# Query, key, gate and up products in two row tiles, value products in one run, and an order table for each engine

## What is computed

```
q, k, v = xn @ Wq.T, xn @ Wk.T, xn @ Wv.T        # 16 heads of 16 features
attn = softmax(causal(q @ k.T) / 4)              # for each head, 512 x 512
s = (attn @ v) @ Wo.T
h = silu(xn @ wg.T / 127) * (xn @ wu.T / 127)    # 768 features, int weights
g = silu(h @ wd.T / 127)
out = x + s * g
```

## Time and profile before

| what | value |
|---|---|
| median of 3 runs | 946.51 us (945.27 to 947.13) |
| span of the profiled execution | 945.8 us |
| PE busy | 914.8 us (97%), 9065 matmuls |
| DVE busy | 707.2 us (75%) |
| ACT busy | 585.8 us (62%) |
| POOL busy | 495.1 us (52%) |
| DMA queue of the kernel, share of 16 engines | 41.8%, 132.47 MB |

### The profile page before, as it was taken

How to read it: one execution, slowest core, us unless ns; L and a number is a source line. 1 busy time by engine, 2 the same in 40 slices (tenths; PEclk the granted TensorE clock), 3 DMA queues, 4 the chain that set the end, 5 groups by cost and what they waited for, 6 DMA issues and landing times.

```text
span 945.8 us, 22760 instructions
## 1 busy us (share of the span) xinstructions
PE 914.8 (97%) x9065; PEld 685.6 (72%) x9065; DVE 707.2 (75%) x950; ACT 585.8 (62%) x796; POOL 495.1 (52%) x681
## 2 busy tenths in 40 slices
PE   3999999999999999999999999999999999999995
PEld 2777767776868777686877868777786867768654
DVE  5985868778696887868788786877778697776823
ACT  5356664757576675756657575665757557575771
POOL 4253553736456464645636455473745547364553
PEclk9999999999999999999999999999999999999999
DMA  6704235353353534535343453534345253543323
GB/s 221 213 25 170 84 116 169 100 198 132 134 164 127 170 106 179 154 125 171 129 151 126 170 152 117 176 132 158 130 148 162 104 185 120 175 131 135 118 93 98
DMA packets 84507, 133.97 MB, mean 142 GB/s; under 512 B 13680, under 2 KB 34928, under 8 KB 84336
## 3 DMA queue, kind: packets, MB, share of 16 engines
q1 hardware_dynamic: 84400, 132.47, 41.8%
HBM read 53.22 MB, written 25.75 MB: 83 GB/s over the span
## 4 chain that ended last, share of the span: by engine, by line
PE 91%; DVE 2%; DMA 2%; POOL 2%; issue 1%; ACT 1%; SPq 0%; POOLq 0%; ACTq 0%; DVEq 0%
PE bank L194 48%; PE values L525 15%; PE bank L434 12%; PE bank L492 11%; PE bank L447 4%; DMA o_reciprocals<-scratch_r 1%; ACT probs L500 1%; DVE row_max L457 1%; PE bank L463 1%; POOL o_compact L566 1%; PE bank L668 0%; DMA scratch_r<-sum_reciprocals 0%; DVE x_in L259 0%; DVE xt_lo L279 0%; DMA sums<-scratch_o 0%
## 5 line engine op out<-in xcount | busy, mean ns | idle before, releaser
L457 DVE TENSOR_REDUCE row_max<-bank 128x2 f32<-128x768 f32 (+3 forms) x352 | 384.9, 1124 | 63.5 <-PE bank L447 60.3
L500 ACT ACTIVATE probs<-bank 128x1024 f32<-128x1024 f32 x320 | 320.4, 1026 | 122.2 <-PE bank L492 120.8
L507 POOL TENSOR_SCALAR_AFFINE_SELECT probs<-probs 128x256 f32<-128x256 f32 (+1 forms) x448 | 194.0, 450 | 275.1 <-ACT probs L500 274.1
L525 PE MATMUL values<-probs,v 128*17 128x512 f32 (+3 forms) x2048 | 166.2, 436 | 0.9 <-POOL probs L507 0.9
L393 POOL TENSOR_TENSOR h_lo<-gated,h_hi 128x512 fp32r<-128x512 f32 x96 | 124.6, 1298 | 74.8 <-ACT h_hi L390 72.7
L434 PE MATMUL bank<-k_stack,q_stack 64*128 64x128 f32 (+3 forms) x1024 | 155.3, 363 | 1.5 <-DVE row_max L457 1.2
L492 PE MATMUL bank<-q_stack,k_stack 64*128 64x512 f32 (+3 forms) x1024 | 142.2, 350 | 1.3 <-DVE row_max L457 0.7
L434 PEld LDWEIGHTS bank<-k_stack,q_stack 64*128 64x128 f32 x1024 | 83.1, 186 | 66.9 <-issue 30.4
L492 PEld LDWEIGHTS bank<-q_stack,k_stack 64*128 64x128 f32 x1024 | 82.9, 186 | 39.1 <-issue 17.3
L366 DVE SCALAR_TENSOR_TENSOR gated<-gated,bank 128x512 f32<-128x512 f32 x96 | 65.8, 685 | 55.4 <-ACT gated L363 55.4
L194 PE MATMUL bank<-xt_hi,wg_hi 128*128 128x256 f32 x384 | 99.3, 293 | 1.6 <-DVE gated L379 1.6
(11 more groups left out here) (123 smaller groups left out, 1624.4 us busy)
## 6 DMA issues: line engine op xcount, KB each, us to landing
k_stack<-qk_hi SPq DMA_DIRECT2D x64, 256.0 KB, 2.5
q_stack<-qk_hi SPq DMA_DIRECT2D x64, 256.0 KB, 2.5
scratch_o<-o SPq DMA_DIRECT2D x64, 256.0 KB, 2.2
x_again<-x SPq DMA_DIRECT2D x16, 512.0 KB, 4.7
k_stack<-qk_lo SPq DMA_DIRECT2D x32, 256.0 KB, 2.5
q_stack<-qk_lo SPq DMA_DIRECT2D x32, 256.0 KB, 2.6
o_compact<-scratch_o SPq DMA_DIRECT2D x32, 256.0 KB
o_reciprocals<-scratch_r SPq DMA_DIRECT2D x32, 256.0 KB
```

Of the source, the lines that this page charges most:

```text
L457: signal(e.tensor_reduce(rows, scores, axis=AX.X, op=ALU.max), "d_sm")
L500: signal(e.activation(PR[:, (SCORES * beta + k) % SLOTS, :, :], both(banks), ACT.Exp, scale=SCALE_S), "d_ex")
L507: last = e.affine_select(out=diag, in_=diag, compare_op=ALU.is_ge, fill=0.0, base=0, pattern=[[0, many], [1, P]], channel_multiplier=-1)
L525: last = nc.tensor.matmul(PVB[32 * c:32 * c + VW, j * P:S], V[par][:, j, 4 * g + c, :], PR[:, (SCORES * beta + 5 * g + kind) % SLOTS, pari ...
```

## The change

1. `qk`, `gg` and `gu` go to row-tile mode. The weights of key and query (`kq`) and of gate and up (`gu`) stand together in one tile: of each 64 features of the input, one matrix has its rows on partitions 0 to 63 and the other on 64 to 127. Each pair makes 64 features of the sum for both, into two banks. The transposed input `xt_hi`, `xt_lo` is needed on both halves: a new unit `xd` copies it across with 4 DMAs of 256 KB for a sequence, and PE waits for them (`s_dup`). A product over 256 features is 4 chunks of 64 in place of 2 of 128. `qa` and `ga` are first parts, `qk` and `gg` second parts of one product.
2. Keys and queries of 8 heads are read from two banks by one ACT and one DVE instruction.
3. `pv` of a group of 4 heads is one run of PE, into a bank of the ring, which now has all 8 banks. `probs` has 7 slots.
4. `q_stack` and `k_stack` are 3 half stacks each in place of 2 whole ones. `mt` transposes in two row tiles.
5. Each engine has its own table of the order of its units.

The core of the diff (the HEAD and TAIL tables and what concerns names and the setup of weights are left out):

```diff
-RING = 7
-SLOTS = 5
+RING = 8
+SLOTS = 7
+STACKS = 3
+CHUNKS = 4
...
-PERIOD = table("""
-    ld 2 0, on 0 0, zr 0 0, ob 0 0, pv 0 11, sm 1 16 45, lt 2 0, st 1 1 01, la 2 0, st 1 2 23, mk 1 16 45, lm 2 0, gg 1 3 6,
-    os 0 0, lc 2 0, gu 1 2 1, gg 1 4 2, st 1 3 34, pv 1 0, st 1 4 56, sm 1 17 01, st 1 5 34, mk 1 17 01, od 0 1, gu 1 3 2,
...
+PERIOD = dict(
+    sp=table("""
+        zr 0 0, lt 2 0, ld 4 0, xr 0 0, lm 3 0, pv 0 1, lc 3 0, od 0 0, or 0 0, ob 0 0, ls 1 2, ls 1 3, mt 1 0, pv 0 2, zr 0 1,
+        xd 2 0, xd 2 1, pv 0 3, od 0 1, or 0 1, ob 0 1, ls 2 0, ls 2 1, pv 1 0, mt 1 1, op 0 0, op 0 1"""),
...
+    act=table("""
+        st 0 8, st 0 9, gg 1 1, v 1 1, hs 1 0, hs 1 1, dn 0 1, pv 0 1, st 0 10, st 0 11, st 0 12, qk 1 1, st 0 13, st 0 14, gg 1 2,
+        st 0 15, mt 1 0, gg 1 3, hs 1 2, os 0 0, pv 0 2, st 0 16, st 0 17, st 0 18, gg 1 4, st 0 19, gg 1 5, lx 2 0, hs 1 3,
+        hs 1 4, st 1 0, hs 1 5, dn 1 0, pv 0 3, st 1 1, v 2 0, st 1 2, st 1 3, st 1 4, st 1 5, qk 2 0, st 1 6, gg 2 0, os 0 1,
+        pv 1 0, mt 1 1, st 1 7"""),
+    dve=table("""
+        la 3 0, gu 1 1, mk 1 0, mk 1 1, mk 1 2, mk 1 3, mk 1 4, dn 0 1, mk 1 5, mk 1 6, mk 1 7, mk 1 8, mk 1 9, or 0 0, qk 1 1,
+        mk 1 10, gu 1 2, mt 1 0, gu 1 3, os 0 0, gu 1 4, mk 1 11, mk 1 12, gu 1 5, lx 2 0, mk 1 13, mk 1 14, dn 1 0, mk 1 15,
+        mk 1 16, mk 1 17, or 0 1, mk 1 18, mk 1 19, qk 2 0, mk 1 20, mk 1 21, os 0 1, gu 2 0, mt 1 1, op 0 0, op 0 1"""),
+    pe=table("""
+        st 0 9 23, ga 1 1 45, gg 1 1, sm 1 0 01, sm 1 1 23, mk 1 0, mk 1 1, sm 1 2 67, mk 1 2, v 1 1 4, dn 0 1 5, sm 1 3 01,
+        sm 1 4 23, sm 1 5 67, mk 1 3, mk 1 4, mk 1 5, pv 0 1 4, st 0 10 01, sm 1 6 23, mk 1 6, sm 1 7 45, mk 1 7, sm 1 8 67,
+        mk 1 8, st 0 11 01, qa 1 1 23, st 0 12 45, sm 1 9 01, mk 1 9, qk 1 1, st 0 13 45, st 0 14 01, ga 1 2 67, gg 1 2,
+        sm 1 10 45, mk 1 10, ga 1 3 23, st 0 15 01, gg 1 3, mt 1 0 45, pv 0 2 6, st 0 16 01, ga 1 4 23, st 0 17 45, st 0 18 67,
+        gg 1 4, st 0 19 01, ga 1 5 45, sm 1 11 67, mk 1 11, gg 1 5, sm 1 12 01, mk 1 12, dn 1 0 2, sm 1 13 01, sm 1 14 67,
+        st 1 0 34, mk 1 13, mk 1 14, pv 0 3 5, st 1 1 01, sm 1 15 34, sm 1 16 67, mk 1 15, mk 1 16, v 2 0 5, st 1 2 01, sm 1 17 23,
+        st 1 3 67, mk 1 17, qa 2 0 45, sm 1 18 01, st 1 4 23, st 1 5 67, mk 1 18, qk 2 0, sm 1 19 23, st 1 6 01, mk 1 19,
+        ga 2 0 67, gg 2 0, sm 1 20 01, mk 1 20, sm 1 21 23, mk 1 21, pv 1 0 5, st 1 7 01, mt 1 1 23, op 0 0 4, op 0 1 7, st 1 8 01"""))
...
+        def u_xd(en, e, beta, par, k, banks, prev):
+            if en == "sp":
+                after(e, ("d_xh", "d_xl")[k], beta, 1)
+                for to, at in (ROWSETS, ROWSETS[::-1]):
+                    e.dma_start(XT[k][to:to + STACK, KT:CHUNKS, :], XT[k][at:at + STACK, 0:KT, :]).then_inc(s_dup, 16)
...
+        def pair_products(banks, at, w, col, xs, chunks, parts):
+
+            for c in chunks:
+                for n, (a, b) in enumerate(parts):
+                    for low, m in zip(ROWSETS, banks):
+                        last = nc.tensor.matmul(PS[:, m, at], r(W[w][a][low:low + STACK, c, col:col + P]), r(XT[b][low:low + STACK, c, xs]),
+                                                start=c == 0 and n == 0, stop=c == CHUNKS - 1 and n == len(parts) - 1)
+            return last
...
+        def u_pv(en, e, beta, par, g, banks, prev):
+            if en == "pe":
+                if g == 0:
+                    after(e, "d_v", beta, 1)
+                prev(e)
+                for part, (done, blocks) in enumerate(((1, 1), (3, 2), (4, 1))):
+                    after(e, "d_mk", beta, 5 * g + done)
...
+            elif en == "act":
                 wait(e, s_ost, 16 * (4 * beta + g))
-                after(e, "f_pv", beta, k)
-                signal(e.activation(O[:], PVB[:], ACT.Copy), "d_ov")
-            elif en == "sp" and part == 2:
+                after(e, "f_pv", beta, 3 * g + 2)
+                signal(e.activation(O[:], PS[:, banks[0], :], ACT.Copy), "d_ov")
```

More of the change, by code:

```diff
@@ L109, in build, with banks_of_units @@
+BRANCH = [kind for kind, *_ in HEAD["pe"]].index("if")
+FIRST = dict(mk="sm", qk="qa", gg="ga", gu="ga")
+STEPS = [HEAD] + [PERIOD] * (B - 3) + [TAIL]
+def banks_of_units():
+    return {(kind, b + ahead, k): banks for b, tables in enumerate(STEPS) for kind, ahead, k, banks in tables["pe"] if banks}
+BANKS = banks_of_units()
 def build(nc, x, xT, wqT, wkT, wvT, woT, wgT, wuT, wdT, out, scratch_o, scratch_r, scratch_m):
@@ L427, in u_sm @@
                         e.wait_ge(s_rows, 32)
-                    elif half == 0 and beta > 1:
-                        wait(e, s_zero, 16 * (beta - 1))
+                    else:
+                        wait(e, s_zero[1 - half], 16 * (beta - 1 + half))
                 prev(e)
@@ L434, in u_sm @@
                         nc.tensor.matmul(PS[:, n, j * keys:(j + 1) * keys],
[L435 to L436 removed]
+                                         r(QS[slot(beta, half)][low:low + STACK, pair % (PAIRS // 2), i * P:(i + 1) * P]),
+                                         r(KS[slot(beta, half)][low:low + STACK, pair % (PAIRS // 2), 0:keys]), start=j == 0, stop=False,
                                          skip_group_check=True)
@@ L462, in u_mt @@
                 prev(e, ("sm", len(MAXIMA) // 2 * (k + 1) - 1))
-                signal(e.transpose(PS[:, banks[0], 0:P], MX[:, k, :], IDF[:]), "f_mt")
+                for low, m in zip(ROWSETS, banks):
+                    last = e.transpose(PS[:, m, 0:STACK], MX[low:low + STACK, k, :], IDF[low:low + STACK, low:low + STACK])
+                signal(last, "f_mt")
             elif en == "act":
@@ L581, in product @@
             def product(j):
-                return PVB[:, 0:E] if halves and j == 1 else PS[:, banks[0], j * E:(j + 1) * E]
+                return PS[:, banks[1], 0:E] if halves and j == 1 else PS[:, banks[0], j * E:(j + 1) * E]
             if en == "pe":
@@ L700, in step, with weight @@
                 UNIT[kind](en, e, b + ahead, (b + ahead) % 2, k, banks, prev)
-                if kind in RELEASED:
+                if en == "pe" and kind in RELEASED:
                     users.update((n, (kind, b + ahead, k)) for n in banks)
+                    if kind == "ga":
+                        users[banks[0]] = ("gt", b + ahead, k)
         stage_p = PR[:].rearrange("p a b c -> p (a b c)")
         stage_g = GATES[:].rearrange("p a t e -> p (a t e)")
+        def weight(name, w, cols, stage, *sources):
+            tiles = W[w][0].shape[1]
+            return name, sources, W[w][0][:, :, cols], W[w][1][:, :, cols], stage.rearrange("p (t n) -> p t n", t=tiles)
@@ L718, in run, with later_steps @@
+        WCOLS = dict(gu1=slice(middle, F), gu0=slice(0, middle))
+        ORDER = [w for w, *_ in WEIGHTS]
+        def later_steps(en, e, first, users):
+            step(en, e, 0, first, users)
+            for b in range(1, B - 1):
+                step(en, e, b, STEPS[b][en], users)
         def run(en, e):
-            users = {}
-            step(en, e, 0, HEAD[:BRANCH], users)
+            first, users = HEAD[en], {}
             if en != "pe":
-                later_steps(en, e, users)
+                later_steps(en, e, first, users)
@@ L723, in run @@
                 return
+            step(en, e, 0, first[:BRANCH], users)
             e.wait_ge(s_flag, 3)
@@ L806, in _ @@
             e.wait_ge(s_zeros, 1)
-            nc.tensor.matmul(PVB[:], ZERO[:, 0:P], ZERO[:], start=True, stop=True).then_inc(s_fixed, 1)
             run("pe", e)
```

366 lines of the change are left out of this document (197 added, 169 removed).

## The result

The changed kernel takes 992.42 us (median of 4 runs, 984.9 to 996.96) against 946.82 for the kernel before in the same job: a ratio of 1.0478, 95% interval 1.0452 to 1.0503. I had predicted 931 with a range of 913 to 949. It is slower, and the forecast was on the wrong side.

The account below looks back on a forecast made before the run. PE was taken as the bound, a step being the sum of its matmul prices. From the profiled 945.8: - 33.8 + 1.5 + 2 + 15 = 930.5, timed runs 0.7 above, so 931 us; range 913 to 949.

Parts of the forecast that it names:

- The prices: PE matmuls: a pair of 256 columns costs 0.12 us, of 512 0.24, like full ones; medians sum to 53.6 a step.
- weights exposed in long runs: Rival, runs of 6 and more pairs: each pays 0.10 us for its weights, adding 192 us: 1120; 2%.
- Instruction supply: Rival, PE in long gate products: only 35 ns an instruction sustained, adding 36 us: 967; 2%.
- row tiles bring nothing: Rival, PE mode changes: leaving a mode costs only where DVE's semaphore is waited for: 945 to 955; 2%, half a draw.
- New waits in a step: PE against the other engines' new tables: waits lose 1.0 us a step, 15 us over 15 steps.
- `op 0 0`: First output product: 14.2 us second-half chain against 13.5 of PE work, wait 0.7 us, between 0.2 and 3.3.
- `sm 1 7`: PE comes 0.1 to 0.2 us before ACT's copy out of bank 4; 0.3 us together with `st 0 11`.
- the reciprocal chain takes over the step: Rival, at `op 0 0`: waits 2.9 there, 3.1 a step, 962; decides from 2.0 a step; 12% for slower.
- xd hidden: Copies of x, 4 DMAs a sequence: wanted 12 us after `gg 1 5`, hidden; without cover about 3 us wait.
- The start: Until the first output product: 29.8 us beyond prices taken over from the kernel before, in an implied 126.9 us.
- The end: Behind the last values: the chain remains, 25 to 28 us to the end.

Follow-up runs that it names:

- version 14: 12 with `gg 1 5` ahead of `sm 1 11` and a new order of the last step: 936.7 us, ratio 0.989.
- Experiment 3: Changed kernel with ACT's split of the first half (`os 0 0`) moved behind the copy `pv 0 2` and exponential `st 0 16`: 977.2 us, ratio 1.034.
- experiment 4: Changed kernel with the output products and the second half's split moved into the start of the next step: 1025.9 us, ratio 1.080.
- Version 1: Changed kernel without the broadcast read of the reciprocals, GpSimd multiplying by ones: 931.0 us, ratio 0.981.
- 13: Kernel before, without the broadcast read of the reciprocals: 942.1 us, ratio 0.995.
- Versions 11: Changed kernel with the output product cut in two and DVE's `gu 2 0` ahead of the second half's split `os 0 1`: 961.9 us, ratio 1.018.
- 12: Versions 11's kernel with the start order of Experiment 6 and ACT's split of the first half behind `st 0 17`: 945.9 us, ratio 0.998.
- Experiment 6: Changed kernel with `tr 0 0, tr 0 1` ahead of the gate and up weights on ACT and DVE at the start: 983.8 us, ratio 1.037.

## Why the prediction was wrong

On the scale of the profiled execution the forecast was 930.5 and the span is 995.0, 64.5 more. By place: until the first output product 140.0 us, where the sum implied 126.9 (96.1 of prices, the 29.8 that the kernel before adds there, 1.0 of wait): 13.1. Thirteen steps 755.0 where 13 times 54.44 was forecast: 47.3. The rest 100.0 against 95.9: 4.1.

**The prices: right.** 116 and 235 ns for pairs of 256 and 512 columns. Without waits a step would be the 53.4 of the sum of medians; the best steps of version 14 take 53.5 to 53.8. The rival "weights exposed in long runs" is out, and with it, once more, what the Trainium skill (TensorE: Matmul & The Clock Gate, section "Part 3: Packing small matmuls") says of weight loads on the same row group: eight pairs in a row on the same two halves took 0.12 each. "Instruction supply" and "row tiles bring nothing" are out by the same rows.

**The step that failed: "New waits in a step".** Forecast 1.0 us, measured 4.6, in these parts (over 13 steps, each against the price of the same neighbours without a wait):

- `op 0 0`: 0.7 forecast, 1.56 measured. The mechanism was right and the chain was mis-sized: 14.2 taken, 15.1 measured. I had sums of 14.6 and 16.8 from the rows and went below both, because the read of the reciprocals looked long for an idle queue. It isn't: 3.6 us from issue to POOL's start with nothing else on the queue (978.79 to 982.41).
- `st 0 18`: not in the sum, 1.34 measured. I priced the chain for the second half, where PE waits for it by name, and not for the first, where ACT waits and PE's bank stands behind ACT. The waits themselves are 15.2 us in the 13 steps; the rest of the 1.34 is in the distances around them. Experiment 3 shows it.
- `v 1 1`: not in the sum, 0.56. DVE's `gu 1 1`, which frees the bank, stands behind `la 3 0`.
- `sm 1 7`: in the sum with 0.3 (together with `st 0 11`), measured 0.36 (0.38 from the mask ahead of it to its first matmul, where other places take 0.03). So this term was about right.
- The clock: not in the sum. What remains of the 4.6 is 0.8, and in the 13 steps 10.2 us of the full clock are missing, also 0.8 a step. Behind the wait at `op 0 0` the granted clock falls to 0.50, the level of 1.2 GHz, and the full products of 256 columns there take 0.22 in place of 0.12 (373.72 to 373.94). Stretches of one us of the changed kernel; PE busy stands behind the length, the granted clock is the third number from the end:

```profile
487.00:488.00 1.00, 0.00 (x0) 0.00 (x0) 0.39 (x1) 1.00 (x2) 0.00 (x0) 1.00 1.00 383
488.00:489.00 1.00, 0.65 (x5) 0.65 (x6) 0.90 (x2) 0.95 (x3) 0.00 (x0) 1.00 0.97 379
489.00:490.00 1.00, 1.00 (x8) 1.00 (x8) 0.97 (x2) 0.40 (x1) 0.00 (x0) 0.59 0.69 262
490.00:491.00 1.00, 1.00 (x6) 1.00 (x6) 0.28 (x2) 0.00 (x0) 0.00 (x0) 0.50 0.00 0
491.00:492.00 1.00, 1.00 (x7) 1.00 (x6) 0.42 (x1) 0.00 (x0) 0.50 (x1) 0.50 0.08 21
492.00:493.00 1.00, 1.00 (x8) 0.86 (x7) 0.00 (x0) 0.00 (x0) 0.77 (x1) 0.70 0.04 12
```

0.41, 0.50, 0.50 and 0.30 are missing, 1.7 us, behind a wait of 1.7. From 139 to 895 us there are 14 first output products. Those with such a stretch had waited 1.7 to 2.6 us, those without one 0.8 to 1.3, but for one of 2.1. A seventh stretch starts at 693.98, behind a wait of 1.96 at `st 0 18`; waits of 2.4 and 1.8 at the same unit have none behind them. (The expectation of experiment 4 speaks of 8 stretches; there are seven.) The mean clock of the span is 0.976, that of the kernel before 0.998.

Version 1 has the same PE table, so the same 684 matmuls of a step can be laid side by side. A step of it is 4.0 us shorter: 1.6 stand ahead of `op 0 0`, 1.4 at `st 0 18`, 0.6 in the output products at the lower clock, and 0.4 in many small places. The waits at `v 1 1` and `sm 1 7` are in both. With them the fastest step of version 1 takes only 53.6, so the 53.4 of the medians is some tenths too high for this table, and the parts listed above carry that error.

**The rival that came true** is "the reciprocal chain takes over the step", which I gave 12% and 962. Its point, 2.0 us a step, and its sign (PE's waits name `o_lo`) were right. Its size was not, 3.1 against 4.6, because it had one half only, and no clock. Experiments 1 and 13 together show that the cause is the place of this chain in the tables: the same DMA is worth 61 us in one kernel and 4.5 in the other. Versions 11, 12 and 14 show it from the other side: the chain is as long as ever (15 us), and with each exchange the kernel gets faster, 961.9, 945.9 and 936.7.

**xd hidden: right.** No wait for `s_dup`; without the copies the waits stay.

**The start: wrong by omission.** I took over the 29.8 us that the kernel before spends there beyond its prices. The new tables turn the gate and up weights ahead of x, and the first wait was 7.28 where it had been 1.41. Experiment 6 gives that wait back (1.41 again). The other 7 us or so of the 13.1 are small waits for reductions and masks; version 14 still has its first output product at 137.8, and I did not settle them.

**The end: nearly right.** From the last values to the end 24.9 us, where 25 to 28 was forecast. The part from 895 us on is 4.1 longer than I allowed, in waits and in the clock behind the output product at 894.95.

## What to carry to other kernels

A round trip through DRAM in a kernel with fixed orders has as many places to be paid as there are engines that wait in it: for each of its stages ask what is queued behind the waiting instruction, and which bank that frees. Take the long rows for its price, not the sum that you would like; a table that covers it by 1 us too little costs more than the 1 us (here 1.6 at the wait itself and 0.6 through the clock, of 4.0 in a step). When an experiment removes a wait and nothing is gained, look for the same landing in another line of the list before giving up the theory: here one exchange of two units on DVE made 42 us of it. And give the same cut to the kernel before: 61 us against 4.5 is what told the place of the chain from its length.

## What was not expected of the hardware

- The granted clock fell to 0.50 for 3.4 us around or behind single PE waits of 1.7 to 2.6 us, with PE otherwise busy: at 6 of 14 output products and once at `st 0 18`. Three other waits of 1.8 to 2.4 us had none.
- The broadcast read of 256 KB took 3.6 us from issue to the start of its user on a quiet queue, 3.8 and 4.7 in the steps (medians of the second and the first half).
- Eight pairs with new weights each on the same two row groups ran at 0.12 us each.
